# Windowed attention on one core: the output transposes move one step later, next to the transposed maxima, and scores and keys alternate

## What is computed

```python
qkv = layernorm(x) @ w_qkv
q, k, v = windows(qkv)                      # B, 16 heads, 16 windows, 128, 32
k_ctx, v_ctx = (previous, own, next window) # 3 * 128 keys, 2 * 128 at the ends
scores = einsum('bhnqe,bhnke->bhnqk', q * scale, k_ctx)
attn = softmax(scores, axis=-1)
out = einsum('bhnqk,bhnke->bhnqe', attn, v_ctx)
```

## Time and profile before

| | us |
|---|---|
| median of three runs | 2947.65 |
| the profiled execution's own time | 2945.01 |
| its span in the profile | 2943.2 |
| mean granted TensorE clock in it | 0.992 |
| TensorE matmul busy | 2872.6 (98%) |
| VectorE busy | 1997.2 (68%) |
| ScalarE busy | 1731.4 (59%) |
| GpSimd busy | 854.8 (29%) |

### The profile page before, as it was taken

How to read it: one execution, slowest core, us unless ns; L and a number is a source line. 1 busy time by engine, 2 the same in 40 slices (tenths; PEclk the granted TensorE clock), 3 DMA queues, 4 the chain that set the end, 5 groups by cost and what they waited for, 6 DMA issues and landing times.

```text
span 2943.2 us, 55585 instructions
## 1 busy us (share of the span) xinstructions
PE 2872.6 (98%) x20380; PEld 2397.3 (81%) x20380; DVE 1997.2 (68%) x3769; ACT 1731.4 (59%) x3385; POOL 854.8 (29%) x715
## 2 busy tenths in 40 slices
PE   8999999999999999989989999999999999999998
PEld 6888888788888888778868888888888888888886
DVE  5333333488888887888868766876768766786664
ACT  3222222367767676665636666866668666676666
POOL 1000000188888888874400000500005000040003
PEclk9999999999999999999989999999999999999999
DMA  6555555677888889959998866986669755795642
GB/s 215 185 172 171 186 188 193 215 189 193 195 197 194 196 196 228 217 178 393 397 386 338 292 207 209 357 308 210 240 209 404 273 203 202 286 399 198 233 136 86
DMA packets 361429, 697.10 MB, mean 237 GB/s; under 512 B 26576, under 2 KB 127056, under 8 KB 361184
## 3 DMA queue, kind: packets, MB, share of 16 engines
q1 hardware_dynamic: 336464, 629.89, 66.4%
q10 hardware_dynamic: 16416, 31.98, 3.1%
q0 software_dynamic: 8304, 31.98, 2.7%
HBM read 525.45 MB, written 167.78 MB: 236 GB/s over the span
## 4 chain that ended last, share of the span: by engine, by line
PE 82%; DMA 6%; DVE 4%; issue 2%; ACT 2%; SPq 2%; POOL 1%; ACTq 0%; DVEq 0%; POOLq 0%
PE a_acc L574 17%; PE e_hid L1394 7%; PE e_hid L1392 7%; PE e_hid L1393 7%; PE e_acc L1409 7%; PE e_acc L1411 7%; PE e_acc L1410 7%; PE a_ps_keys L642 5%; PE a_ps_score L625 5%; PE a_ps_out L671 5%; DMA a_q_st<-a_max_rows 3%; DMA a_gate_att<-o_scratch 3%; PE a_ps_out L679 1%; DVE e_part L1782 1%; PE a_turn L569 1%
## 5 line engine op out<-in xcount | busy, mean ns | idle before, releaser
L1782 DVE SCALAR_TENSOR_TENSOR e_part<-e_ring,e_g_cols,e_part 128x512 f32<-128x512 f32 x896 | 647.6, 777 | 4.6 <-DMA e_ring<-mix_rows 2.2
L491 DVE TENSOR_REDUCE a_neg_max<-a_ps_score 128x1 f32<-128x384 f32 (+1 forms) x1024 | 491.8, 526 | 64.0 <-PE a_ps_score L625 53.0
L329 POOL TENSOR_TENSOR a_total<-a_probs 128x512 f32<-128x512 f32 x256 | 324.1, 1283 | 593.3 <-ACT a_probs L421 593.2
L421 ACT ACTIVATE a_probs<-a_ps_keys 128x384 f32<-128x384 f32 (+1 forms) x1024 | 427.1, 478 | 53.7 <-PE a_ps_keys L642 27.3
L1806 DVE TENSOR_TENSOR e_u_lo<-e_u,e_u_hi 128x512 fp32r<-128x512 f32 x256 | 180.0, 703 | 373.8 <-ACT e_u_hi L1540 373.6
L1536 ACT ACTIVATE e_u<-e_hid,e_mb 128x512 f32<-128x512 f32 x256 | 176.9, 691 | 433.8 <-PE e_hid L1394 421.2
L1265 POOL TENSOR_SCALAR e_var<-e_moments 128x4 f32<-128x4 f32 x15 | 6.7, 447 | 1275.5 <-DVE e_moments L1818 1274.8
L642 PE MATMUL a_ps_keys<-a_q_st,a_k_st 97*128 97x384 f32 (+1 forms) x1024 | 314.4, 349 | 16.5 <-DMA a_q_st<-a_max_rows 15.3
L625 PE MATMUL a_ps_score<-a_k_st,a_q_st 96*128 96x384 f32 (+1 forms) x1024 | 327.6, 358 | 2.7 <-DVE a_neg_max L491 2.5
L339 POOL TENSOR_TENSOR a_total<-a_total,a_probs 128x512 f32<-128x512 f32 x224 | 286.1, 1279 | 63.6 <-ACT a_probs L421 61.2
L471 DVE TENSOR_TENSOR a_qk<-a_acc,a_qk 128x512 fp32r<-128x512 f32 x128 | 88.0, 690 | 308.0 <-ACT a_qk L370 308.0
(11 more groups left out here) (158 smaller groups left out, 6506.0 us busy)
## 6 DMA issues: line engine op xcount, KB each, us to landing
e_ring<-mix_rows SPq DMA_DIRECT2D x558, 512.0 KB, 5.4
qk_scratch<-a_qk SPq DMA_DIRECT2D x128, 512.0 KB, 3.2
a_k_st<-qk_scratch SPq DMA_DIRECT2D x180, 256.0 KB, 4.4
a_q_st<-qk_scratch SPq DMA_DIRECT2D x180, 256.0 KB, 4.5
v_scratch<-a_v SPq DMA_DIRECT2D x64, 256.0 KB, 3.0
a_v_sb<-v_scratch SPq DMA_DIRECT2D x64, 256.0 KB, 4.9
o_scratch<-a_out SPq DMA_DIRECT2D x128, 128.0 KB, 3.0
x_scratch<-a_gate_x POOLq DMA_DIRECT2D x16, 1024.0 KB, 10.2
```

The costliest lines, as they stand in the source:

```text
L329: add = pool.tensor_tensor(total[:, g % 2, i], p[0], p[1], ALU.add)
L421: act.activation(probs[:, m % PROBS, h, 0:(hi - lo) * WIN], ps_keys[x % TRIO][:, 0:(hi - lo) * WIN], ACT.Exp, scale=SCALE).then_inc(exp_do ...
L491: dve.tensor_reduce(neg_max[:, g % 2, i, h:h + 1], ps_score[y % TRIO][:, 0:(hi - lo) * WIN], AX_X, ALU.max, negate=True).then_inc(reduced, 1)
L1782: dve.scalar_tensor_tensor(out=part[:, n % 2, half, :], in0=ring[:, slot, :], scalar=g_cols[:, b, e:e + 1], in1=so_far, op0=ALU.mult, op1= ...
```

## The change

TensorE's order in a step becomes: s0 k0 s1 k1 s2 k2, values(T-2), sums(T-2), `turn_out(T-3)`, along, `turn_max(T+2)`, s3 k3 s4 k4 s5 k5 s6 k6 s7 k7. `normalise` and `store` stay at their places in VectorE's and SyncE's lists and handle step T-3 instead of T-2. In step 128 both outputs 125 (at the new place) and 126 (at the end of the step) are turned, in step 129 output 127. `turn_max` asks for one normalised step less, as it runs at most one step ahead of it.

```diff
+        def turned_in(T):
+
+            steps = [T - LAG - 1] * (T <= STEPS) + [T - LAG] * (T >= STEPS)
+            return [g for g in steps if there(g)]
...
-                if there(T - LAG):
-                    store(T - LAG)
+                for g in turned_in(T):
+                    store(g)
...
-                if there(T - LAG):
-                    normalise(T - LAG)
+                for g in turned_in(T):
+                    normalise(g)
...
-                turned = g - AHEAD - LAG + 1
+                turned = g - AHEAD - LAG
...
             for T in range(STEPS + LAG):
-                scores(T, [0])
-                all_keys(T, [0])
-                scores(T, [1])
-                all_keys(T, [1, 2])
-                scores(T, [2])
+                for x in range(3):
+                    scores(T, [x])
+                    all_keys(T, [x])
                 if there(T - LAG):
                     values(T - LAG)
                     sums(T - LAG)
+                if T <= STEPS and there(T - LAG - 1):
+                    turn_out(T - LAG - 1)
                 along(T)
                 if there(T + AHEAD - 1):
                     turn_max(T + AHEAD - 1)
-                scores(T, [3])
-                all_keys(T, [3])
-                scores(T, [4])
-                all_keys(T, [4, 5])
-                scores(T, [5, 6])
-                all_keys(T, [6])
-                if there(T - LAG):
+                for x in range(3, UNITS):
+                    scores(T, [x])
+                    all_keys(T, [x])
+                if T >= STEPS and there(T - LAG):
                     turn_out(T - LAG)
-                all_keys(T, [7])
-                scores(T, [7])
```

## The result

Four runs of the changed kernel took 2978.24 us in the median (2976.62 to 2980.34), against 2946.88 (2942.09 to 2952.69) for four runs of the kernel before. The ratio is 1.0098, 95% interval 1.0078 to 1.0117: 1% slower. The forecast was 2990, with a range of 2966 to 3018. The profiled execution took 2976.6 us, with a span of 2974.8: 31.6 us more than before.

A forecast was written before the change was run, and what follows sets the result against it. The bound was taken as a loop of hand-overs between TensorE and VectorE, nearly equal, VectorE late once per step. Loop +51.4, shorter waits -9, end +1: +43 us, 2991 against the median 2947.65, stated as 2990; range 2966 to 3018.

The forecast's parts named there:

- The hold at the scores: After k6: the 0.45 us a step TensorE could gain is all taken by score units waiting for VectorE's reduces.
- The gain of k2 and s2: k2 and s2 change places ahead of values: values still start at 3.62 us after turn_max, gain 0.
- The step in eight with 256 columns: One step in eight, scores of 256 columns: VectorE not the limit, values at 3.1 instead of 3.43, gain 0.34 us.
- the 0.06 of the sum: Another step of the eight, keys of 256 columns: waits cost 0.06 us more.
- The block between sums and turn_max: turn_out's four weight loads between sums and turn_max lengthen each step by 0.44 us, bounds 0.21 and 0.60.
- Rival A: turn_out's block between sums and turn_max hides in part: 0.21 to 0.33 us instead of 0.44, 2972 us; chance 0.10.
- Waits that become shorter: Keys' 26 waits for the DMA of the maxima each shrink by 0.35 us in the longer step: 9 us less.
- The end: Step 128 has one turn_out and one normalise more: 1 us.
- B: TensorE alone sets the step, which becomes faster: 5.37 instead of 5.50 us, whole 2931 us; chance 0.04.
- D: No effect: turn_out's 0.45 us saved and its 0.44 paid with no wait between, 2946 us; chance 0.02.
- C: The clock falls, as TensorE would idle in four pieces, 0.6 us a step: 3020 us; chance 0.06.

The follow-up runs named there:

- short maxima: VectorE's maxima taken over the first 256 of 384 columns: changed kernel 2932.89 us (ratio to before 0.9940), kernel before 2947.16 us (0.9976).
- The alternation alone: Kernel before with only scores and keys alternating (s0 k0 to s7 k7), turn_out(T-2) at its old place: 2944.32 us, ratio 0.9979.
- the end mended: Changed kernel with outputs 124 and 125 both turned, normalised and stored in step 127, 126 in step 128: 2975.74 us, ratio 1.0084.

## Why the prediction was right

**The hold at the scores** was the step that decided, and it held in its numbers. Forecast were s7 at 1.64, s0 at 2.11, s1 at 2.57 and s2 at 3.04 after turn_max, and values at 3.62; measured 1.63, 2.19, 2.61, 3.02 and 3.57. (s0 came 0.08 later than its reduce explains, and the profile names no engine for it.) The short maxima show the cause. Score loads waited 0.64 us a step (44.0/69); 0.5 or more was forecast.

**The gain of k2 and s2, put at 0** as the values start where they did: right as a sum. What the alternation does alone was measured as nothing, too.

**The step in eight with 256 columns** was forecast with values at 3.1; they came at 3.10. Its step is 5.40 instead of 5.33, all others grew by 0.37 to 0.44. The 0.44 is the step with keys of 256 columns, against 0.37 to 0.39 in six others: the 0.06 of the sum.

**The block between sums and turn_max** was put at 0.44, between 0.21 and 0.60. It measured 0.42: from its first transpose 0.165 to the second, 0.11 to the product, 0.03 to its second pass and 0.11 to turn_max. That the total came within 0.02 is partly luck, as four equal loads of 0.11 were forecast and two of the terms were off in opposite directions (+0.055 and -0.08). The gap of 0.20 stayed ahead of the block, once. The Trainium skill, "TensorEngine Tiling (Array Packing)", Key Properties, says that a change of the tiling mode drains the engine. The trace agrees, with one gap of 0.20 before L694 and none before L655. The Trainium skill, "TensorE: Matmul & The Clock Gate", Part 3, says that a load can be pulled ahead of matmuls in flight. Behind the strips this was not at work here: L694's load was not earlier than its matmul (both at 980.56). Rival A falls.

**Waits that become shorter** was the term most off: 9 us forecast, 14.1 fewer in the waits for that DMA (22.7 to 8.6) and 16.8 in the loop. I had cut each wait by 0.35. But store also comes 0.21 us earlier relative to turn_max, and the DMA of the maxima is issued 0.27 us earlier, at 0.68 instead of 0.95 after it (medians over steps 8 to 95). I had named the first and counted neither. How the 14.1 divide between this and the longer step is not shown. The alternation alone issues that DMA as early, at 0.70, with the old step, and its keys waited 17.4. The term also scatters: with the end mended, which leaves the loop as it is, the keys waited 12.5 instead of 8.6.

**The end** was put at 1 us and measured 4.9. The step that failed is "Step 128 has one turn_out and one normalise more". I had counted the instructions and not what stands between in VectorE's list: normalise(125) moved behind the gate stage's work in step 127, and turn_out(126) and the last values wait for it.

**In sum**: 44.3 where 51.4 + 0 was forecast, since the block is 0.02 smaller and the values start 0.04 earlier; -16.8 instead of -9; +4.9 instead of +1. The first two errors, 7.1 and 7.8 us, go one way and the third, 3.9 us, goes the other, which by luck makes the total look better than its terms; 2990 was 12 us too high. Against the profiled execution of before the forecast was +43, measured +31.6.

**The other rivals.** B and D needed scores that are not held; they were held 256 times in 69 steps. It is B's world that the short maxima made: there the two orders are equal. C did not happen in the steady part: the clock granted from 700 to 1100 us is 1.00. Behind it the clock fell in both kernels, in the changed one less:

```profile
1150.00:1200.00 50.00, 44.12 (x644) 38.12 (x648) 42.40 (x102) 31.22 (x73) 39.20 (x33) 0.97 1.05 248
```

```profile
1150.00:1200.00 50.00, 47.40 (x672) 37.58 (x671) 38.79 (x97) 31.85 (x77) 39.87 (x33) 1.00 1.00 235
1200.00:1250.00 50.00, 48.67 (x662) 38.14 (x661) 40.33 (x100) 32.16 (x75) 40.30 (x34) 0.94 0.94 221
```

The first of these lines is of the kernel before, whose stretch from 1200 us had 0.93; the other two are of the changed one. The changed kernel lost the clock once more at the end, during 5.99 us without a matmul, behind which two transposes took 0.66 us instead of 0.44. (B's chance stands at 0.04 in the list and at 0.03 in the closing sum of the range, which changes nothing.)

## What to carry to other kernels

Where two engines hand work to and fro, ask for each place in a step whether it lies between the hand-over and its answer. Work there is free as long as the other engine is slower, work behind the answer costs its full length; moving 0.42 us from the first kind of place to the second cost 0.35 a step. Not all of it reaches the time: 44.3 us of longer steps became 27.5 us of loop, since waits for other things shrank meanwhile. Before rebalancing, count the chains of nearly equal length (here VectorE's reduces, TensorE's issue, ScalarE's exponentials, SyncE's queue). TensorE's hold at s6 is 0.1 us a step; filling it with turn_out bought nothing, and taking it away with short maxima bought 0.1 us a typical step and nothing sure in the time. And if a step is moved by one round of a loop, look at the last rounds by hand, for what else was hung into the list between.

## What the runs showed of the hardware that was not expected

In the changed kernel the first of two transposes behind the strips is followed by the second after 0.165 us; in the kernel before, between scores and keys, it was 0.11. The two passes of the product with 8 columns start only 0.03 us apart in both kernels, though each has a weight load of 128 columns, so counting 0.11 for each load overstates such a pair by 0.08.
